# The Mamba-2 skip term moved from TensorE to VectorE and GpSimd, and product steps placed anew

## The chip, the cores and the metric

The kernel runs on one core of a Trainium2 chip. The metric is device time in microseconds (us) of one execution, the median of several runs. The core has TensorE (matmul, PE in the profile; its weight loads are PEld), VectorE (DVE), ScalarE (ACT), GpSimd (POOL) and SyncE (SP, which here only issues DMAs). TensorE writes its results to PSUM, eight banks here, and every other engine but GpSimd can read them there.

## The reference, cut to what matters

Two layers follow each other on 4096 tokens of width 256. The change lies in the first: a graph product (a 4096 x 4096 matrix of weights, computed from `dist_matrix`, times messages) and then a Mamba-2 block.

```python
weights = jnp.where(dist_matrix < CUTOFF, jnp.exp(-(1.0 / r - 1.0 / mu) ** 2 / (2.0 * sigma * sigma)), 0.0)
x = x + weights @ (z @ W + B)                       # the product of the first layer
...
zxbcdt = x @ W_in                                   # z, xBC and dt
xBC = jax.nn.silu(conv)                             # xh, Bmat, Cmat
...
Y = (Y_diag + Y_off + xh * D[:, None]).reshape(Bsz, L, D_INNER)
Y = Y * jax.nn.silu(z)
Y = Y * jax.lax.rsqrt(jnp.mean(Y * Y, axis=-1, keepdims=True) + EPS) * norm_w
return (Y @ W_out) @ W_lin + b_lin
```

The term `xh * D[:, None]` is the skip: each of the 512 channels of the convolved input times one constant of its head, added to what the recurrence gives.

## The kernel before

The tokens are worked in 8 blocks of 512 (`ib`), each block of the recurrence in 4 chunks of 128 tokens (`s`). The first layer overlaps three things in each block's time, in an order written out by hand (`order_a`, which every engine follows):

- `ssd(ib)`, the recurrence of block ib in 62 steps, with the output projection, a norm and the messages of the next layer behind it;
- `pre_a(ib + 1)`, norm, input projection and convolution of the next block, 55 steps;
- `product_a(ib + 2)`, the product for the block after that, 64 steps ("p") of one matmul each on TensorE. Its weights are made elsewhere ("w"): ScalarE takes a logarithm and two exponentials, VectorE does lines 1146 and 1153 on tiles of 128x1024, each line two at a time. Six tiles `wgt` form a ring.

Blocks 0 to 5 carry all 64 product steps. Block 6 carries 24 and block 7 carries 32 steps of the next layer's product, whose tiles need no such work. TensorE's "p" steps stand where `FILLS` puts them (pairs of an ssd step and a number of product steps ahead of it), and the rest are spread evenly up to ssd step 58:

```python
fill = [ssd_at[i] - 1e-6 for i, n in FILLS for _ in range(n)]
at += [(x, "p") for x in fill + spread(n_fill - len(fill), 0.02, ssd_at[SEND])]
```

One chunk of the recurrence has two parts, and on each engine `inner(s + 1)` stands ahead of `outer(s)`.

- `inner(s)`: TensorE transposes the convolved input into a PSUM bank `X` (785) and makes B transposed and B C in another (789, 791). VectorE takes `X` times dt into `xdt` (1251), copies `bn` (1254) and masks `cbm` (1256). ScalarE makes the decays `E` of 8 heads; GpSimd makes `xdec` (2190) and multiplies `E` by `cbm` (2195, its result is waited for as `M`).
- `outer(s)`: TensorE multiplies C by the state h0 (807, `Yo`), B by xdec (812, `St`), the four 128x128 blocks of the convolved input by diagonal matrices `diagD` that hold D (817, into `Y`), and adds E times xdt for 8 heads to the same bank (823). VectorE scales `Yo` into `tmp` (1266), adds `St` to `hd` for the new state h0 (1271), adds `Y` to `tmp` (1275) and multiplies by the gate z (1278); ScalarE squares that with a sum (1660). GpSimd makes `hd`, the decayed state (2207), from h0.

The state is a chain: 807 of chunk s + 1 waits for 1271 of chunk s, and GpSimd's 2207 of chunk s + 1 too. After the last chunk ScalarE makes the norm's factors `rms`, VectorE scales by them (1288, 1292), TensorE transposes (840) and projects (849).

PSUM banks are given out in rings in the order of use: `pre_a` has two banks, ps2 and ps3, so that each of its uses waits until the use two before it has been read. On TensorE, `pre_a` writes for each m an input part x (753, 755) and a gate part z (760, 762); ScalarE copies each out. Line 745 is the dt projection of `pre_a(ib + 1)`; it waits for the normed input `xc` (VectorE, 1201) and stands once in a block. GpSimd's 2153 adds the two halves of a later block's input, once a block. In the first rounds VectorE also writes `Wc` (1320) from a combination of two weight matrices (875).

## Time and profile before

| | us |
|---|---|
| median of 3 runs | 2359.17 |
| lowest, highest | 2358.28, 2360.71 |
| profiled execution, span of its instructions | 2358.5 |
| TensorE busy in the span | 2189.1 |
| VectorE, ScalarE, GpSimd busy | 1803.0, 1566.7, 1146.6 |

The span of the profiled execution is 0.67 us below the median of the runs. Times of the trace count from the span's start. The first layer's blocks run from about 230 to 1050 us; the second layer takes the rest. Busy time on TensorE is the union of its matmuls, whose modelled ends overlap: one product matmul, two instructions here, starts every 0.86 us, though each lasts 0.59. A block in the steady part is shown below by the stretch from one L745 at 459.5 us to the next at 571.9 us; the blocks around it repeat it.

### The profile page before, as it was taken

What the parts mean: (1) busy time and instruction counts of PE and PEld (TensorE: products, weight loads), DVE (VectorE), ACT (ScalarE), POOL (GpSimd) and SP (SyncE); (2) the same over time, 40 slices, a digit from 0 to 9 for tenths busy, and PEclk for the clock granted to TensorE, in tenths of its full rate; (3) what the DMA queues carried; (4) which work ended last, traced back from release to release, by engine and by line L of the source; (5) the groups of instructions that cost most, each with busy time, mean ns of one, the idle gap of its engine ahead of it and who ended that gap; (6) DMA issues with size and microseconds to landing.
All of it is one profiled execution on the core that took longest, in us unless ns stands there. A gap on an engine that the chain in (4) does not pass through costs nothing.

```text
span 2358.5 us, 26231 instructions
## 1 busy us (share of the span) xinstructions
PE 2189.1 (93%) x8900; PEld 1393.1 (59%) x8900; DVE 1803.0 (76%) x2083; ACT 1566.7 (66%) x2541; POOL 1146.6 (49%) x928
## 2 busy tenths in 40 slices
PE   7999999999999999989999999998999987787998
PEld 4544545555555556456766666676766664444886
DVE  5666767777777765324999998999989998996665
ACT  5577686777686845425676767677676868775444
POOL 2101322222231313213988888888988888890000
PEclk9999999999999999999999999999999999898999
DMA  6243332323232323233323232323323221312121
GB/s 234 72 134 102 108 116 90 125 96 122 87 125 88 119 90 134 83 107 109 131 93 125 90 125 89 117 99 107 117 100 125 90 83 43 117 36 98 36 81 45
DMA packets 117495, 241.22 MB, mean 102 GB/s; under 512 B 8770, under 2 KB 66370, under 8 KB 116978
## 3 DMA queue, kind: packets, MB, share of 16 engines
q1 hardware_dynamic: 108290, 207.14, 26.4%
q0 software_dynamic: 8528, 31.36, 3.8%
q8 instruction: 71, 1.16, 0.2%
q10 hardware_dynamic: 544, 1.05, 0.1%
q14 instruction: 62, 0.51, 0.1%
HBM read 219.20 MB, written 20.32 MB: 102 GB/s over the span
## 4 chain that ended last, share of the span: by engine, by line
PE 65%; ACT 10%; POOL 10%; DVE 10%; issue 5%; DMA 0%; ACTq 0%; DVEq 0%; POOLq 0%
PE ps L685 13%; PE ps L727 10%; POOL dB L2306 6%; PE ps L971 5%; DVE h L1473 3%; PE ps L849 2%; PE ps L823 2%; PE ps L955 2%; POOL acc L2288 2%; PE ps L709 2%; ACT ps L1659 2%; ACT L1657 1%; POOL du L2302 1%; PE ps L755 1%; PE ps L753 1%
## 5 line engine op out<-in xcount | busy, mean ns | idle before, releaser
L1473 DVE TENSOR_TENSOR_SCAN h<-ps,hst,dB 128x512 f32<-128x512 f32 x512 | 636.9, 1270 | 59.0 <-ACT ps L1659 50.5
L2306 POOL TENSOR_TENSOR dB<-du,bc 128x512 f32<-128x512 f32 x512 | 648.0, 1287 | 61.6 <-DVE h L1473 59.1
L685 PE MATMUL ps<-wgt,msg 128*128 128x512 f32 x1024 | 489.0, 598 | 2.1 <-DVE xb L1181 2.1
L1659 ACT ACTIVATE ps<-dt,cols 128x512 f32<-128x512 f32 x512 | 351.9, 692 | 181.1 <-DVE h L1473 178.8
L727 PE MATMUL ps<-raw,msg 128*128 128x256 f32 x1792 | 436.3, 379 | 0.9 <-ACT hb L1659 0.9
L971 PE MATMUL ps<-consts,h 128*128 128x128 f32 x2048 | 318.9, 281 | 70.7 <-DVE acc L1435 38.0
L971 PEld LDWEIGHTS ps<-consts,h 128*128 128x128 f32 x2048 | 251.6, 144 | 224.8 <-DVE acc L1435 73.4
L727 PEld LDWEIGHTS ps<-raw,msg 128*128 128x128 f32 x1792 | 324.0, 190 | 74.1 <-issue 42.1
L685 PEld LDWEIGHTS ps<-wgt,msg 128*128 128x128 f32 x1024 | 190.0, 192 | 206.2 <-issue 204.6
L1659 ACT ACTIVATE wgt<-wgt 128x1024 f32<-128x1024 f32 x256 | 257.9, 1046 | 51.9 <-DVE wgt L1146 50.5
L2288 POOL TENSOR_TENSOR acc<-acc,part 128x512 f32<-128x512 f32 x174 | 226.4, 1301 | 59.7 <-ACT part L1659 58.3
L1146 DVE SCALAR_TENSOR_TENSOR wgt<-wgt 128x1024 f32<-128x1024 f32 x128 | 174.4, 1403 | 54.6 <-ACT wgt L1659 54.6
L1435 DVE SCALAR_TENSOR_TENSOR acc<-ps,Ct,acc 128x512 f32<-128x512 f32 x267 | 193.6, 725 | 5.3 <-PE ps L971 5.2
L1153 DVE SCALAR_TENSOR_TENSOR wgt<-raw,wgt 128x1024 f32<-128x1024 f32 x128 | 167.3, 1348 | 17.9 <-ACT wgt L1659 17.9
L1659 ACT ACTIVATE wgt<-raw 128x1024 f32<-128x1024 f32 x128 | 129.0, 1045 | 24.1 <-PE ps L685 23.9
L2195 POOL TENSOR_TENSOR E<-E,cbm 128x1024 f32<-128x1024 f32 x32 | 81.4, 2545 | 108.4 <-ACT E L1659 108.3
L2226 POOL DMA_DIRECT2D tmp_x<-xb x8 | 5.6, 696 | 254.5 <-DVE xb L1298 254.5
L1659 ACT ACTIVATE part<-ps,Ct 128x512 f32<-128x512 f32 x174 | 117.8, 677 | 1.7 <-PE ps L971 1.5
L2313 POOL TENSOR_TENSOR sq<-sq 128x512 f32<-128x512 f32 x7 | 9.0, 1289 | 207.8 <-ACT sq L1659 207.8
L1660 ACT ACTIVATE tmp<-z 128x512 f32<-128x512 f32 x32 | 20.2, 630 | 130.8 <-DVE z L1278 130.8
L1659 ACT ACTIVATE g<-ps,b 128x512 f32<-128x512 f32 x64 | 43.1, 685 | 84.4 <-PE ps L1052 79.5
L1225 DVE SCALAR_TENSOR_TENSOR cc<-xbc,cols,cc 128x512 f32<-128x512 f32 x120 | 93.6, 780 | 3.1
(320 smaller groups left out, 3589.9 us busy)
## 6 DMA issues: line engine op xcount, KB each, us to landing
raw<-in_adjT SPq DMA_DIRECT2D x256, 512.0 KB, 3.4
bc<-tmp_bc SPq DMA_DIRECT2D x64, 512.0 KB, 4.6
E<-tmp_bc POOLq DMA_DIRECT2D x32, 512.0 KB, 4.1
xb<-in_xT POOLq DMA_DIRECT2D x8, 512.0 KB, 4.1
tmp_x<-xb POOLq DMA_DIRECT2D x8, 512.0 KB, 4.2
x<-tmp_x SPq DMA_DIRECT2D x8, 512.0 KB, 5.8
tmp_x<-x SPq DMA_DIRECT2D x8, 512.0 KB, 4.8
msg<-in_W SPq DMA_DIRECT2D x4, 1024.0 KB, 10.6
```

What stands on the lines that cost most here:

```text
L685: x = e.matmul(P[d][:, :], msg[:, j, d * 128:(d + 1) * 128], wgt[g % NW][:, l, :], start=j == 0, stop=j == NJ - 1)
L727: x = e.matmul(P[0][:, 256 * d:256 * d + 256], msg[:, j, d * 128:(d + 1) * 128], quarters(g)[:, l, :], start=j == 0 and d == 0, stop=j == ...
L971: i = e.transpose(b.ps[:, m * 128:(m + 1) * 128], hr[n % 3][:, m, s * 128:(s + 1) * 128], ident)
L1146: e.scalar_tensor_tensor(wgt[i % NW][:, :, :], wgt[i % NW][:, :, :], -2.0, wgt[i % NW][:, :, :], ALU.add, ALU.mult).then_inc(S("q"), 1)
L1153: e.scalar_tensor_tensor(wgt[i % NW][:, :, :], raw[i % 4][:, :, :], 1.0, wgt[i % NW][:, :, :], ALU.is_lt, ALU.mult).then_inc(S("wgt"), 1)
L1225: e.scalar_tensor_tensor(c, xbc[:, m, k:k + TB], col("cw0", 4 * m + k), c, ALU.mult, ALU.add).then_inc(S("conv"), 1)
L1435: e.scalar_tensor_tensor(acc[:, s, :], b.ps[:, :], c, acc[:, s, :], ALU.mult, ALU.add).then_inc(b.evac, 1)
L1473: e.tensor_tensor_scan(hr[n % 3][:, m, :], PS[4 + k % 2].t[:, :], dBr[k % 4][:, :], hst[:, n % 16, m:m + 1], ALU.mult, ALU.add).then_inc(S ...
L1659: return e.activation(out, in_, func, bias=bias, scale=scale)
L2195: e.tensor_tensor(E[c % 3][:, :, :], E[c % 3][:, :, :], cbms[s % 2][:, None, :].broadcast_to([128, 8, 128]), ALU.mult).then_inc(S("M"), 1)
L2288: e.tensor_tensor(acc[:, s, :], acc[:, s, :], part[HANDED[j] % 2][:, :], ALU.add).then_inc(S("summed"), 1)
L2306: e.tensor_tensor(dBr[k % 4][:, :], du[:, m, :], bcr[i % 3][:, n % 2, :], ALU.mult).then_inc(S("dB"), 1)
```

## The change

The skip no longer goes through TensorE. VectorE multiplies `X` in PSUM by a row `Drow` (128x512, D in every partition) into one of two tiles `skips`, in `inner(s)` ahead of `xdt`. GpSimd adds `tmp` to it in `outer(s)`, after `hd`, and waits for VectorE's 1266 to do so. VectorE's addition of `Y` then takes `skips` in place of `tmp` and waits for GpSimd. TensorE starts `Y` with the E matmuls. `Drow` is made once: one matmul of ones by the diagonal matrices and one copy, in the first rounds. The broadcast row of the messages' bias gets its own tile and DMA, whose room is used for the second skip tile later. `FILLS` puts 23 product steps at fixed places, where it put 16. One semaphore of the last stage is merged into another with the same waits.

```diff
-        rows = sb(cA, "rows", [128, NROW])
-        Bbc, dtb, Abc = rows[:, 0:256], rows[:, 256:288], rows[:, 288:296]
-        diagD = sb(cA, "diagD", [128, 4, 128])
+        rows = sb(cA, "rows", [128, NROW - D])
+        dtb, Abc = rows[:, 0:32], rows[:, 32:40]
+        Drow = sb(cA, "Drow", [128, 512])
...
+        skips = [skip0, sb(cA, "skip1", [128, 512])]
+        diagD = skip0[:, :].rearrange("p (m c) -> p m c", m=4)
...
-        FILLS, SEND, WFIRST, WLAST, EVAC, PREND = ((5, 3), (7, 2), (8, 2), (25, 2), (30, 2), (38, 2), (50, 2), (57, 1)), 58, 0.04, 0.925, 0.97, 0.95
+        FILLS, SEND, WFIRST, WLAST, EVAC, PREND = ((5, 3), (7, 2), (8, 3), (25, 2), (30, 2), (32, 2), (38, 4), (50, 3), (57, 2)), 58, 0.04, 0.925, 0.97, 0.95
... (TensorE, outer)
-                    w.wait_ge(S("setup"), 5)
                     w.wait_ge(Y.evac, Y.n - 1)
-                    for m in range(4):
-                        e.matmul(Y.ps[:, m * 128:(m + 1) * 128], cc[:, m, ts_], diagD[:, m, :], start=m == 0, stop=False,
-                                 skip_group_check=True)
                     yield
                     w.wait_ge(S("M"), 4 * ib + s + 1)
... (TensorE, first rounds, behind the four matmuls of Wc)
+                    b = drow_use()
+                    w.wait_ge(S("setup"), 5)
+                    w.wait_ge(b.evac, b.n - 1)
+                    e.matmul(b.ps[:, :], one, skip0[:, :], start=True, stop=True).then_inc(b.full, 1)
... (VectorE, inner)
+                    if c < 2:
+                        w.wait_ge(drow_use().evac, drow_use().n)
+                    e.tensor_tensor(skips[s % 2][:, :], X.ps[:, :], Drow[:, :], ALU.mult)
                     e.tensor_tensor(heads(xd[:, :]), heads(X.ps[:, :]), dt[:, 8 * s:8 * s + 8, None].broadcast_to([128, 8, 64]),
                                     ALU.mult).then_inc(X.evac, 1)
... (VectorE, outer)
-                    w.wait_ge(Yo.evac, Yo.n)
-                    e.tensor_tensor(tmp[:, :], tmp[:, :], Y.ps[:, :], ALU.add).then_inc(Y.evac, 1)
+                    w.wait_ge(S("skip"), c + 1)
+                    e.tensor_tensor(tmp[:, :], skips[s % 2][:, :], Y.ps[:, :], ALU.add).then_inc(Y.evac, 1)
... (VectorE, first rounds, behind the four writes of Wc)
+                    b = drow_use()
+                    w.wait_ge(b.full, b.n)
+                    e.tensor_copy(Drow[:, :], b.ps[:, :]).then_inc(b.evac, 1)
... (GpSimd, first DMAs)
-            e.dma_start(rows[:, :], t["rows"].broadcast_to([128, NROW])).then_inc(S("d_rows"), 16)
+            e.dma_start(rows[:, :], t["rows"][:, D:NROW].broadcast_to([128, NROW - D])).then_inc(S("d_rows"), 16)
+            e.dma_start(Bbc[:, :], t["rows"][:, 0:D].broadcast_to([128, D])).then_inc(S("d_rows"), 16)
... (GpSimd, outer, behind hd)
-                    yield from [None] * 5
+                    yield from (None, None)
+                    Yo = outer_use(ib, s, 0)
+                    w.wait_ge(Yo.evac, Yo.n)
+                    e.tensor_tensor(skips[s % 2][:, :], skips[s % 2][:, :], tmp[:, :], ALU.add).then_inc(S("skip"), 1)
+                    yield from (None, None, None)
```

TensorE around chunk 1 of a steady block, before. `ps2` is written by 770 and 771 (sums of dt); `ps3` is written by 753 (here the first half of the second input part of `pre_a`), and `ps7` is chunk 1's `Y`:

```order
L812 MATMUL ps6<-xdec1,bn1 128x512
L685 MATMUL ps0<-wgt3,msg 128x512
L770 MATMUL ps2<-sm1,consts 128x32 x3
L771 MATMUL ps2<-consts,sm1 128x128
L817 MATMUL ps7<-diagD,cc0 128x128 x4
L685 MATMUL ps1<-wgt3,msg 128x512
L753 MATMUL ps3<-xc,Win 128x512
L823 MATMUL ps7<-xdt1,E0 128x64 x8
```

The same place now (lines shifted by the change: 685 is 694, 753 is 762, 823 is 828):

```order
L821 MATMUL ps6<-xdec1,bn1 128x512
L779 MATMUL ps2<-sm1,consts 128x32 x3
L780 MATMUL ps2<-consts,sm1 128x128
L694 MATMUL ps1<-wgt3,msg 128x512
L762 MATMUL ps3<-xc,Win 128x512
L694 MATMUL ps0<-wgt3,msg 128x512
L828 MATMUL ps7<-xdt1,E0 128x64 x8
L764 MATMUL ps3<-xc,Win 128x512
```

Between the state's matmul of chunk 1 (812, now 821) and the input part (753, now 762) one product step and the diagonal matmuls are gone.

TensorE around chunk 2 and the state matmul of chunk 3 (807, now 816), before:

```order
L812 MATMUL ps7<-xdec0,bn0 128x512
L685 MATMUL ps0<-wgt0,msg 128x512
L817 MATMUL ps4<-diagD,cc0 128x128 x4
L685 MATMUL ps1<-wgt0,msg 128x512
L685 MATMUL ps0<-wgt0,msg 128x512
L685 MATMUL ps1<-wgt0,msg 128x512
L823 MATMUL ps4<-xdt0,E1 128x64 x8
L685 MATMUL ps0<-wgt1,msg 128x512
L807 MATMUL ps5<-hs0,cc0 128x512
```

And now:

```order
L821 MATMUL ps7<-xdec0,bn0 128x512
L694 MATMUL ps0<-wgt5,msg 128x512
L694 MATMUL ps1<-wgt5,msg 128x512
L694 MATMUL ps0<-wgt0,msg 128x512
L828 MATMUL ps4<-xdt0,E1 128x64 x8
L694 MATMUL ps1<-wgt0,msg 128x512
L694 MATMUL ps0<-wgt0,msg 128x512
L694 MATMUL ps1<-wgt0,msg 128x512
L816 MATMUL ps5<-hs0,cc0 128x512
L694 MATMUL ps0<-wgt1,msg 128x512
```

Four product steps stood between 812 and chunk 2's E matmuls and one between these and the state matmul of chunk 3; now three and three.

GpSimd from chunk 3's `xdec` to the first load of the next block, before:

```order
L2190 TENSOR_TENSOR xdec1<-xdt1,ecd 128x512
L2167 DMA tmp_bc<-turned 32x128
L2195 TENSOR_TENSOR E2<-E2,cbm1 128x1024
L2207 TENSOR_TENSOR hd<-hs0,ecd 64x512 x2
L2153 TENSOR_TENSOR rr<-xb1 128x512
L2161 DMA E0<-tmp_bc 128x1024
```

And now (2190 is 2206, 2195 is 2211, 2207 is 2223, 2153 is 2169; 2228 is the new addition):

```order
L2206 TENSOR_TENSOR xdec1<-xdt1,ecd 128x512
L2183 DMA tmp_bc<-turned 32x128
L2211 TENSOR_TENSOR E2<-E2,cbm1 128x1024
L2223 TENSOR_TENSOR hd<-hs0,ecd 64x512
L2228 TENSOR_TENSOR skip0<-skip0,tmp 128x512
L2223 TENSOR_TENSOR hd<-hs0,ecd 64x512
L2228 TENSOR_TENSOR skip1<-skip1,tmp 128x512
L2169 TENSOR_TENSOR rr<-xb1 128x512
L2177 DMA E0<-tmp_bc 128x1024
```

Each `hd` is followed by an addition into a skip tile; the last `hd` and the sum of the halves (2169) now stand behind it.

## Rows read from the trace of the kernel before

**Rows 1.** The page: busy shares, and TensorE's busy tenths in 40 slices.
```profile
PE 2189.1 (93%) x8900; PEld 1393.1 (59%) x8900; DVE 1803.0 (76%) x2083; ACT 1566.7 (66%) x2541; POOL 1146.6 (49%) x928
...
PE   7999999999999999989999999998999987787998
```

**Rows 2.** By stretch: length; busy us of PE, PEld, DVE, ACT, POOL; granted clock; DMA.
```profile
353.50:465.90 112.40, 110.16 (x387) 59.35 (x386) 83.73 (x101) 84.01 (x131) 27.63 (x22) 1.00 0.33 108
...
907.20:1044.00 136.80, 126.04 (x499) 72.61 (x498) 58.62 (x91) 51.53 (x117) 32.22 (x28) 0.99 0.22 74
```

**Rows 3.** Groups by line on TensorE: count, busy, mean ns, idle before.
```profile
L685 PE MATMUL ps<-wgt,msg 128*128 128x512 f32 x1024 | 489.0, 598 | 2.1 <-DVE xb L1181 2.1
...
L817 PE MATMUL ps<-diagD,cc 128*128 128x128 f32 x256 | 33.8, 275 | 0.0
```

**Rows 4.** TensorE in order of time, end of steady block: start, length, [idle].
```profile
541.25 1.13 PE L634 MATMUL ps<-tmp,consts 128*128 128x512 f32 x2 [1.14 <-DVE tmp L1303]
...
552.84 3.72 PE L861 MATMUL ps<-W,z 128*128 128x256 f32 x16 [1.02 <-DVE z L1312]
...
565.66 6.17 PE L685 MATMUL ps<-wgt,msg 128*128 128x512 f32 x14
571.91 1.95 PE L745 MATMUL ps<-Win,xc 128*128 128x8 f32 x16
```

**Rows 5.** The chain that ended last: start, length, work of each piece.
```profile
459.53 1.95 PE ps L745 x16
...
480.52 0.89 PE ps L817 x8
...
569.73 0.60 DVE xdt L1251
...
570.72 1.14 DVE xc L1201
...
571.91 1.95 PE ps L745 x16
```

**Rows 6.** VectorE in order of time, steady block 459.5 to 571.9.
```profile
493.87 1.53 DVE L1225 SCALAR_TENSOR_TENSOR cc<-xbc,cols,cc 128x512 f32<-128x512 f32 x2
495.32 0.68 DVE L1266 TENSOR_TENSOR tmp<-ps,ecd 128x512 f32<-128x512 f32 x1
496.23 4.47 DVE L1153 SCALAR_TENSOR_TENSOR wgt<-raw,wgt 128x1024 f32<-128x1024 f32 x2 [0.22 <-ACT wgt L1659]
500.62 0.67 DVE L1271 TENSOR_TENSOR hs<-hd,ps 64x512 f32<-64x512 f32 x1
...
506.09 2.36 DVE L1146 SCALAR_TENSOR_TENSOR wgt<-wgt 128x1024 f32<-128x1024 f32 x2 [0.19 <-ACT wgt L1659]
...
515.17 0.49 DVE L1288 TENSOR_SCALAR z<-z,rms 128x512 f32<-128x512 f32 x1 [1.26 <-ACT rms L1659]
```

**Rows 7.** GpSimd in order of time, same block.
```profile
494.84 2.78 POOL L2195 TENSOR_TENSOR E<-E,cbm 128x1024 f32<-128x1024 f32 x1 [2.79 <-ACT E L1659]
497.60 2.02 POOL L2207 TENSOR_TENSOR hd<-hs,ecd 64x512 f32<-64x512 f32 x1
...
502.48 1.27 POOL L2153 TENSOR_TENSOR rr<-xb 128x512 f32<-128x512 f32 x1
```

**Rows 8.** ScalarE, then three TensorE rows, same block.
```profile
479.92 0.58 ACT L1659 ACTIVATE z<-ps 128x512 f32<-128x512 f32 x1
...
482.11 1.02 PE L753 MATMUL ps<-xc,Win 128*128 128x512 f32 x2
...
503.66 1.02 PE L807 MATMUL ps<-hs,cc 128*128 128x512 f32 x2
...
517.50 0.60 PE L840 MATMUL ps<-consts,z 128*128 128x128 f32 x4
```

**Rows 9.** VectorE: a collision in block 6, then the first rounds.
```profile
926.55 3.83 DVE L1225 SCALAR_TENSOR_TENSOR cc<-xbc,cols,cc 128x512 f32<-128x512 f32 x1
...
37.25 0.48 DVE L1320 TENSOR_SCALAR Wc<-ps,cols 128x256 f32<-128x256 f32 x1 [1.16 <-PE ps L875]
37.65 2.35 DVE L1153 SCALAR_TENSOR_TENSOR wgt<-raw,wgt 128x1024 f32<-128x1024 f32 x2
```

More of the change, by code:

```diff
@@ L219, in build @@
         hd = sb(cA, "hd", [64, 512])
+        skip0 = sb(cA, "skip0", [128, 512])
+        cM = ExitStack()
+        Bbc = sb(cM, "Bbc", [128, D])
+        cM.close()
+        skips = [skip0, sb(cA, "skip1", [128, 512])]
+        diagD = skip0[:, :].rearrange("p (m c) -> p m c", m=4)
         cA.close()
@@ L271, in build @@
         lane_b = (ccs[0][:, 2:4, :], ccs[0][:, 4:6, :], xdecs[1][:, :])
-        ring_a, ring_b = Ring(PS[2:5], 6 * NB // 2), Ring(PS[5:8], 6 * NB // 2 + 4)
+        ring_a, ring_b = Ring(PS[2:5], 6 * NB // 2), Ring(PS[5:8], 6 * NB // 2 + 5)
         prod = [Ring(PS[0:1], 3 * NB + 1), Ring(PS[1:2], NB + 1)]
@@ L283, in message_use @@
             if ib % 2:
-                return ring_b.use(ib // 2 * 6 + (4 if ib > 1 else 0) + i)
+                return ring_b.use(ib // 2 * 6 + (5 if ib > 1 else 0) + i)
             return ring_a.use(ib // 2 * 6 + i)
@@ L288, in combined_use, with drow_use @@
             return ring_b.use(6 + m)
+        def drow_use():
+            return ring_b.use(10)
         def pre_use(ib, i):
@@ L436, in build @@
         over_a = [(prod[1].use(NB).full, prod[1].use(NB).n), (ssd_use(NB - 1, 27).evac, ssd_use(NB - 1, 27).n), (ssd_use(NB - 1, 31).evac, ssd_use(NB - 1, 31).n),
-                  (S("hd"), 4 * NB), (S("M"), 4 * NB), (S("xdec"), 4 * NB), (S("halo"), NB + 1),
+                  (S("hd"), 4 * NB), (S("M"), 4 * NB), (S("skip"), 4 * NB), (S("xdec"), 4 * NB), (S("halo"), NB + 1),
                   *((S(f"d_x2_{b}"), 16 * len(range(b, NB, 3))) for b in range(3)), (S("d_m2"), 16 * (NB - 2))]
@@ L822, in outer @@
                     for h in range(8):
-                        i = e.matmul(Y.ps[:, h * 64:(h + 1) * 64], Es[:, h, :], xd[:, h * 64:(h + 1) * 64], start=False,
-                                     stop=h == 7, skip_group_check=True)
+                        i = e.matmul(Y.ps[:, h * 64:(h + 1) * 64], Es[:, h, :], xd[:, h * 64:(h + 1) * 64], start=True,
+                                     stop=True)
                     i.then_inc(Y.full, 1)
@@ L1087, in mean_of_bias @@
                 b = end_use(2)
-                w.wait_ge(S("b2c"), 1)
+                w.wait_ge(S("b2c"), 2)
                 w.wait_ge(b.evac, b.n - 1)
@@ L1134, in messages @@
                 yield
-                w.wait_ge(S("d_rows"), 16)
+                w.wait_ge(S("d_rows"), 32)
                 for s in range(4):
@@ L1138, in messages @@
                     w.wait_ge(b.full, b.n)
-                    e.tensor_tensor(msg[:, 4 * ib + s, :], b.ps[:, 0:256], Bbc, ALU.add).then_inc(b.evac, 1)
+                    e.tensor_tensor(msg[:, 4 * ib + s, :], b.ps[:, 0:256], Bbc[:, :], ALU.add).then_inc(b.evac, 1)
                     yield
@@ L1574, in second_matrices @@
                 w.wait_ge(b_tw.evac, b_tw.n)
-                e.tensor_scalar(b2[:, 0, :], b2[:, 0, :], tw[:, 0:1], None, ALU.mult).then_inc(S("b2a"), 1)
-                w.wait_ge(S("b2a"), 1)
+                e.tensor_scalar(b2[:, 0, :], b2[:, 0, :], tw[:, 0:1], None, ALU.mult).then_inc(S("b2c"), 1)
+                w.wait_ge(S("b2c"), 1)
                 e.scalar_tensor_tensor(b2c[:, :], b2[:, 1, :], tw[:, 1:2], b2[:, 0, :], ALU.mult, ALU.add).then_inc(S("b2c"), 1)
@@ L1663, in _ @@
             e.dma_start(spots[1], t["xT"][:, :, TB:2 * TB]).then_inc(S("d_x0"), 16)
-            w.wait_ge(S("d_rows"), 16)
+            w.wait_ge(S("d_rows"), 32)
             act(Abc, Abc, ACT.Exp).then_inc(S("Aexp"), 1)
```

## The prediction

> **What bounds the kernel now.** I read the page first: TensorE is busy in 93% of the span and in nine tenths or more of nearly every slice of the first layer [rows 1]. Then busy time by stretch: in one steady block TensorE is busy 110.16 of 112.40 us at granted clock 1.00, VectorE 83.73, ScalarE 84.01, GpSimd 27.63 [rows 2]. Then TensorE in order of time: in that block it waits in two places only, 1.14 and 1.02 us [rows 4]. By those views TensorE is the bound of blocks 0 to 5, and matmuls taken from it should come off the block one for one. The chain of waits adds a warning: the block's anchor, L745, starts 112.38 us after the last one, and right behind VectorE's 1201 (570.72 + 1.14 = 571.86), while the product steps ahead of it end at 565.66 + 6.17 = 571.83 [rows 4, 5]. There two bounds coincide. So I walk VectorE, ScalarE and GpSimd through a block too, since each works in order and gains nothing by the change.
>
> **What comes off TensorE.** L817 has 256 instructions, 8 per chunk [rows 3], and one chunk's eight hold the chain for 0.89 us [rows 5]. That is 3.56 us per block, and 28.5 us for all eight blocks. FILLS takes nothing away: 64 steps remain 64. From the first output transposes (840) to the block's end the order is the same as before, so a block's length changes by what happens ahead of 840, and by L745.
>
> **VectorE ahead of L745.** The new multiply stands ahead of `xdt`, and reads one operand from PSUM as 1251 does, so I take 1251's 0.60 us on the chain [rows 5], plus its 0.05 of spacing: 0.65. For chunk 1 it comes between 1146 and 1201, with nothing to hide it, as the sum above shows. Cost: 0.65 us per block, six times. For chunk 0 VectorE waits for the transposes and ScalarE takes `xc` later; I cost that at nothing, at most another 0.65 if that cover is gone.
>
> **GpSimd's addition.** It reads two SBUF tiles of 128x512; its nearest row is 2153's, 1.27 us [rows 7]. GpSimd has the time, but not VectorE: 1153's pair lasts 4.47 us in [rows 6] and 2.35 in [rows 9]. In that stretch GpSimd's 2195 runs to 497.62 and 2207 takes 2.02 us [rows 7] for 64x512, and 4.47 is what one tile after 2195, then 2207, then the other tile would take: 497.6 - 496.23 + 1.1 + 1.0 + 1.1 = 4.57. Meanwhile 1266, with a PSUM operand, keeps its 0.68 beside 2195 [rows 6, 7]. So operations with all inputs in SBUF take turns on the two engines, and those with a PSUM input don't. Each addition may then hold VectorE up by 0 to 1.27 us: 0 where VectorE is at a PSUM read, 1.27 where it wants the turn.
>
> By the Trainium skill ("SBUF — State Buffer", "Who interferes with whom") GpSimd and a VectorE instruction with two SBUF inputs exclude each other for the whole instruction, and the first to issue holds the ports. The trace agrees in the 4.47. If each of the four additions of a block held VectorE up in full, that would be 5.1 us per block of VectorE's time by my 1.27.
>
> **The first uncovered wait.** TensorE now reaches the second input part (753) sooner: the diagonals of chunks 0 and 1 are gone (2 x 0.89) and two product steps stand elsewhere (2 x 0.86; seven of them take 6.01 us in [rows 4]), in all 3.5 us: 482.11 - 3.5 = 478.6 [rows 8]. It writes a bank whose former content ScalarE copies out from 479.92 to 480.5 [rows 8]. That copy stands at the end of ScalarE's own run of work, which begins behind VectorE's chunk 0 and doesn't see TensorE. So 753 waits to 480.5 or 480.8, some 2 us. From 753 to the state matmul of chunk 3 (807) TensorE had 21.55 us (503.66 - 482.11); there a diagonal set goes and a product step comes, 21.5. So 807 can't start before about 502.0, against 503.66 before. At most 1.6 us of 3.56 is left by then.
>
> **The second.** 807 also needs the state from 1271, which ended at 500.62 + 0.67 = 501.3 [rows 6]. What lies ahead of it on VectorE gets longer. The two multiplies of chunks 2 and 3 take 0.65 each, the first of them inside a wait. With the wait for GpSimd's addition at chunk 1, VectorE is 0.8 us late at the pair 1225 (493.87 before, so 494.7), and ScalarE, less delayed, lets GpSimd's 2195 come at 495.2 (494.84 before) [rows 6, 7]. Before, 2195 came while the second 1225 ran, and waited: 2.78 in place of 2.36. Now it comes while the first runs, and would go ahead of the second. Then 1225's second waits 2.35 us, 1266 follows at 498.5, and the pair 1153 takes its turns with `hd` and with the new addition: 1271 ends near 503.6. If the second 1225 still goes first, 1271 ends near 502.3. So 807 starts between 502.3 and 503.6, and the wait for the state eats nearly all the 3.5 us. The three product steps put there have been worked off by then.
>
> **The third.** Behind it `hd` of chunk 3 waits for the addition of chunk 2, and the addition of chunk 3 and the sum of the halves fall on the pair 1146 (506.09, 2.36 alone [rows 6]), which grows by up to 2 x 1.27. VectorE's scaling 1288 (515.17) moves to 517.9 to 518.4, and 840 (517.50) to 518.3 to 518.9 [rows 6, 8]. TensorE gets there at 518.2, so it waits up to 0.7 us. As the new order holds one product step more ahead of 840 and one less behind it (0.86 us), TensorE behind the second transposes stands where it stood, or up to 0.6 us later.
>
> **Sum for blocks 0 to 5.** Per block 0.65 (L745) and -0.05 to +0.6: +0.6 to +1.25 us. I take +0.9, the middle, because the turn of 1225 and 2195 hangs on 0.3 us. Six blocks: +5.4.
>
> **Blocks 6 and 7, and the start.** These have no `wgt` work, so VectorE is light (58.62 of 136.8 us, [rows 2]) and some of TensorE's gain arrives. In block 6 the state of chunk 3 hangs on a 1225 that takes 3.83 us beside GpSimd [rows 9], and stays there; behind it the last diagonal and the moved steps give about 1.8. In block 7 each chunk hangs on E, GpSimd and the state: about 1.0. In the first rounds the extra matmul (0.86) and copy (0.48, as 1320) stand between 1320 and 1153 on VectorE [rows 9]: +1.3. The second DMA of the bias row is issued by GpSimd 0.54 us later than the first and is hidden by the load of the inputs; 0.5 if not. The merged semaphore costs nothing.
>
> Sum: 5.4 - 1.8 - 1.0 + 1.3 = +3.9 us against the profiled span, 2358.5, gives 2362.4; the median of runs lies 0.67 above it: **2363.1 us**.
>
> **Rivals.**
> - *The gain comes through in part.* The turns fall well, 1271 ends near 501.3 and 840 isn't late. Then ScalarE's copy is the bound: -1.6 + 0.65 = -0.95 per block, or -2 if VectorE's chunk 0 also ends 1 us sooner. Six times, with -1.5 for the rest: 2351.9, down to 2346. For it: every wait so far was small, and the race is close. Against: the walk needs all turns to fall one way.
> - *The gain comes through whole.* TensorE is the only bound: -28.5 + 1.3, so 2332. Against: ScalarE's copy at 479.92, which nothing in the change moves.
> - *Slower by turns lost.* In [rows 9] a 1225 waits for two GpSimd operations in a row, 3.83 us. If the additions at chunks 2 and 3 do this to VectorE in each steady block, the loss there is one more operation, 1.27 to 2.4 us above mine: per block +2.2 to +3.3, six times +13 to +20, so 2371 to 2378. It decides as soon as 1271 of chunk 2 ends later than 503.7. By the rule cited above the holder keeps the ports for an instruction, and says nothing of who is next; it makes this no less likely.
> - *The change doesn't do what it says*: TensorE waits elsewhere for as long, and the length is the same to 1 us: 2359. That is inside my forecast's range.
>
> **How the numbers follow.** About 0.2% (4.7 us) can be told from no change. Forecast and its near side (2358 to 2367) 0.52; in part 0.24; whole 0.04; turns lost 0.20. Faster than 2354.5: 0.04 and most of the second case, 0.22. Slower than 2363.9: turns lost and nearly half of the forecast, 0.42. The rest, 0.36, is within 0.2%. The range of 8 in 10 leaves out the whole gain, the far end of the partial one and the far end of turns lost: 2350 to 2372.
>
> **What the profile after would show.** No 128x128 group of `diagD`; 32 multiplies of 0.69 and 32 additions of 1.27 or more. TensorE less busy per steady block by 3.5 us but not shorter: waits at the second input part (2 us, for ScalarE), at the state matmul of chunk 3 (1 to 2 us more, for 1271), at the first output transposes, and 0.6 at L745 for 1201. 1153 and 1225 longer in the mean. I am wrong if the distance of two L745 is under 111.5 us: then VectorE had slack that I didn't see, or the turns fell well; and wrong the other way if it is over 114.

## The result, and the profile after

| | before | after |
|---|---|---|
| median of 4 runs, us | 2359.78 | 2368.14 |
| lowest to highest, us | 2358.28 to 2360.71 | 2364.64 to 2370.41 |
| span of the profiled run, us | 2358.5 | 2362.7 |
| second L745 (L754 after) to the last, us | 666.9 | 675.4 |
| one steady block, us | 112.37 | 113.8 |

The ratio is 1.0037, with an interval of 1.0025 to 1.0049: the change makes the kernel 0.37% slower. The profiled run of after was its fastest, 2364.64 us; that its span is 2362.7 is because a run's time is 1.8 to 2.1 us above the span of its instructions, here and in every run below. In after the lines have moved: L745 is L754, L753 is L762, L807 is L816, L840 is L845, L1271 is L1283, L1201 is L1210, L1153 is L1162, L1225 is L1234, L2195 is L2211, L2207 is L2223. The new ones are L1262 (VectorE's multiply) and L2228 (GpSimd's addition).

The page of after, the busy shares and the shares of the chain; [rows 1] answer to the first line:

```profile
PE 2172.5 (92%) x8646; PEld 1364.9 (58%) x8646; DVE 1867.0 (79%) x2116; ACT 1567.6 (66%) x2541; POOL 1190.9 (50%) x961
...
PE 49%; ACT 15%; DVE 14%; POOL 14%; issue 7%; DMA 1%; DVEq 0%; ACTq 0%; POOLq 0%
```

TensorE's share of the chain is down to 49%, from 65% on the page of before; the other three engines have 43% between them, before 30%.

After, by stretch from one L754 to the next (us, busy us and count of PE, PEld, DVE, ACT, POOL, granted clock, DMA); they answer to [rows 2]:

```profile
235.49:348.61 113.12, 107.19 (x353) 55.45 (x353) 93.28 (x105) 84.00 (x132) 33.10 (x26) 1.00 0.33 107
462.42:576.26 113.84, 108.70 (x353) 56.19 (x353) 93.53 (x105) 84.17 (x132) 33.09 (x26) 0.99 0.32 107
576.26:690.02 113.76, 108.98 (x352) 56.14 (x352) 93.24 (x105) 84.15 (x132) 33.08 (x26) 0.98 0.32 107
```

TensorE has 32 records less in a block (353 against 385), yet its busy time fell by 1.2 to 1.5 us in the later two, and by nearly 3 us only in the first. The first is the one whose granted clock stayed at 1.00.

After, TensorE's groups by line between 235.49 and 910.84 (count, busy us, mean ns, idle before and what ended it):

```profile
L762 PE MATMUL ps<-xc,Win 128*128 128x512 f32 x60 | 33.0, 633 | 9.4 <-ACT z L1674 9.4
...
L816 PE MATMUL ps<-hs,cc 128*128 128x512 f32 x48 | 27.5, 657 | 3.4 <-DVE hs L1283 3.4
...
L845 PE MATMUL ps<-consts,z 128*128 128x128 f32 x96 | 13.8, 276 | 0.7
...
L754 PE MATMUL ps<-Win,xc 128*128 128x8 f32 x97 | 11.9, 257 | 3.4 <-DVE xc L1210 3.4
```

The same four had no idle time of note before (0.4 us in all, at L745). They wait where the prediction put the waits: for ScalarE's `z` copy, for the state, for `xc`. After, one steady block in order of time (start, length, [idle before]), TensorE first, then VectorE, then GpSimd; they answer to [rows 4], [rows 6] and [rows 7]:

```profile
576.26 1.95 PE L754 MATMUL ps<-Win,xc 128*128 128x8 f32 x16 [0.68 <-DVE xc L1210]
...
579.00 1.83 PE L694 MATMUL ps<-wgt,msg 128*128 128x512 f32 x2
580.63 1.91 PE L821 MATMUL ps<-xdec,bn 128*128 128x512 f32 x2
...
598.15 1.10 PE L762 MATMUL ps<-xc,Win 128*128 128x512 f32 x2 [0.96 <-ACT z L1674]
...
620.76 1.12 PE L816 MATMUL ps<-hs,cc 128*128 128x512 f32 x2 [0.86 <-DVE hs L1283]
...
635.81 1.09 PE L845 MATMUL ps<-consts,z 128*128 128x128 f32 x8
```

```profile
576.12 4.54 DVE L1162 SCALAR_TENSOR_TENSOR wgt<-raw,wgt 128x1024 f32<-128x1024 f32 x2
...
612.26 3.51 DVE L1234 SCALAR_TENSOR_TENSOR cc<-xbc,cols,cc 128x512 f32<-128x512 f32 x2
...
616.29 3.82 DVE L1162 SCALAR_TENSOR_TENSOR wgt<-raw,wgt 128x1024 f32<-128x1024 f32 x2
620.04 0.67 DVE L1283 TENSOR_TENSOR hs<-hd,ps 64x512 f32<-64x512 f32 x1
```

```profile
577.22 2.36 POOL L2211 TENSOR_TENSOR E<-E,cbm 128x1024 f32<-128x1024 f32 x1 [1.43 <-ACT E L1674]
579.55 2.02 POOL L2223 TENSOR_TENSOR hd<-hs,ecd 64x512 f32<-64x512 f32 x1
...
612.81 2.41 POOL L2211 TENSOR_TENSOR E<-E,cbm 128x1024 f32<-128x1024 f32 x1 [2.19 <-ACT E L1674]
...
616.63 1.26 POOL L2228 TENSOR_TENSOR skip<-skip,tmp 128x512 f32<-128x512 f32 x1
```

At 612 the pair L1234, 1.53 us in [rows 6], lasts 3.51, because L2211 comes at 612.81 and goes ahead of the second; L1162 behind it takes its turns with `hd` and with the addition. That is the late branch of the race at the second wait. At 576.12 the same happened where I had not looked: the multiply of 0.6 us ahead of L1162 lets GpSimd's L2211 in between its two instructions, and the pair takes 4.54 us, 2.35 before ([rows 9] have one that runs alone). Version 5 below, which leaves the multiply out, has 2.35 there again. By the Trainium skill ("SBUF — State Buffer", "Who interferes with whom") a VectorE instruction with two SBUF inputs contends with a GpSimd instruction that reads SBUF; the 4.54 us agree.

**What I did not foresee** is in the two rows behind L754. A pair of 128x512 matmuls takes 1.02 us in [rows 8]; here two pairs take 1.83 and 1.91. After, TensorE alone by short stretches: us, busy, granted clock, DMA:

```profile
578.70:582.40 3.70, 3.70 (x7) 0.55 0.54 158
483.50:487.00 3.50, 3.18 (x4) 0.51 0.02 5
```

The granted clock stands at 0.50, the 1.2 GHz level, for some 3.4 us; below this is called a fall. Through blocks 0 to 5, after has five such falls, one in each stretch from the second to the sixth: three start 1 to 3 us behind the 0.68 us wait at L754 (350, 579, 692), two right behind a wait of 2.2 us at L762 (483, 825). Before has none between 235 and 902.

### The profile page after: what moved, and what is told of

It reads as the page before. It is cut to its first block, busy times and chain, and to the rows that moved or that the text cites. A ratio compares the mean times of both kernels' runs of the same rounds, so it can differ in the third digit from the quotient of the medians.

```text
span 2362.7 us, 25802 instructions
## 1 busy us (share of the span) xinstructions
PE 2172.5 (92%) x8646; PEld 1364.9 (58%) x8646; DVE 1867.0 (79%) x2116; ACT 1567.6 (66%) x2541; POOL 1190.9 (50%) x961
## 4 chain that ended last, share of the span: by engine, by line
PE 49%; ACT 15%; DVE 14%; POOL 14%; issue 7%; DMA 1%; DVEq 0%; ACTq 0%; POOLq 0%
PE ps L736 10%; PE ps L694 7%; POOL dB L2326 6%; PE ps L980 5%; ACT wgt L1674 3%; DVE h L1488 3%; ACT E L1674 3%; PE ps L854 2%; DVE wgt L1162 2%; PE ps L964 2%; POOL E L2211 2%; POOL acc L2308 2%; ACT ps L1674 2%; ACT L1672 2%; DVE wgt L1155 2%
## 5 line engine op out<-in xcount | busy, mean ns | idle before, releaser
L1155 DVE SCALAR_TENSOR_TENSOR wgt<-wgt 128x1024 f32<-128x1024 f32 x128 | 196.4, 1575 | 46.3 <-ACT wgt L1674 46.3
L1162 DVE SCALAR_TENSOR_TENSOR wgt<-raw,wgt 128x1024 f32<-128x1024 f32 x128 | 176.0, 1416 | 10.6 <-ACT wgt L1674 10.2
L2211 POOL TENSOR_TENSOR E<-E,cbm 128x1024 f32<-128x1024 f32 x32 | 76.2, 2382 | 100.5 <-ACT E L1674 100.5
L1234 DVE SCALAR_TENSOR_TENSOR cc<-xbc,cols,cc 128x512 f32<-128x512 f32 x120 | 105.6, 880 | 3.1
```

The lines of the kernel that those rows point to most:

```text
L1155: e.scalar_tensor_tensor(wgt[i % NW][:, :, :], wgt[i % NW][:, :, :], -2.0, wgt[i % NW][:, :, :], ALU.add, ALU.mult).then_inc(S("q"), 1)
L1162: e.scalar_tensor_tensor(wgt[i % NW][:, :, :], raw[i % 4][:, :, :], 1.0, wgt[i % NW][:, :, :], ALU.is_lt, ALU.mult).then_inc(S("wgt"), 1)
L1234: e.scalar_tensor_tensor(c, xbc[:, m, k:k + TB], col("cw0", 4 * m + k), c, ALU.mult, ALU.add).then_inc(S("conv"), 1)
L2211: e.tensor_tensor(E[c % 3][:, :, :], E[c % 3][:, :, :], cbms[s % 2][:, None, :].broadcast_to([128, 8, 128]), ALU.mult).then_inc(S("M"), 1)
```

## Experiments

Two theories at the start. **A**: VectorE, ScalarE and GpSimd bound a block as soon as TensorE is relieved, so little of the 28.5 us could come through. **B**: TensorE is the bound and the change's own additions eat the gain. Single questions came with them: multiply or addition, the placement, the clock. All lengths below are of one block, L745 (L754) to the next, in the one execution of each version that was profiled. "At a full clock" means a granted clock of 1.00 throughout the block. Versions 1, 2, 5, 6 and 9 leave the skip, or a part of it, out of the result.

**1. The removal alone.**

```diff
-                    for m in range(4):
-                        e.matmul(Y.ps[:, m * 128:(m + 1) * 128], cc[:, m, ts_], diagD[:, m, :], start=m == 0, stop=False,
-                                 skip_group_check=True)
...
-                        i = e.matmul(Y.ps[:, h * 64:(h + 1) * 64], Es[:, h, :], xd[:, h * 64:(h + 1) * 64], start=False,
-                                     stop=h == 7, skip_group_check=True)
+                        i = e.matmul(Y.ps[:, h * 64:(h + 1) * 64], Es[:, h, :], xd[:, h * 64:(h + 1) * 64], start=True,
+                                     stop=True)
```

> The kernel before without its diagonal matmuls (L817) and with nothing in their place, all steps placed as before; the recurrence's skip is left out of the result. It asks what the removal alone could ever give. Theory A (the chain of ScalarE's z copy, VectorE's convolution and GpSimd's products bounds a block soon after TensorE is relieved): a block goes from 112.37 us to about 110.8, total near 2348 us, range 2344 to 2353. Rival B (TensorE alone bounds the stage): the whole 28.5 us come back, total near 2331 us. Rival C (waits take all of it): within 2 us of 2359.

Measured: 2336.14 us (2334.63 to 2338.74), ratio 0.9909 (0.9892 to 0.9925). One block by stretch, then its TensorE and ScalarE rows:

```profile
559.80:668.94 109.14, 106.84 (x353) 55.67 (x353) 83.30 (x101) 84.04 (x132) 27.97 (x22) 1.00 0.34 111
```

```profile
580.19 0.58 ACT L1656 ACTIVATE z<-ps 128x512 f32<-128x512 f32 x1
```

```profile
580.82 1.12 PE L753 MATMUL ps<-xc,Win 128*128 128x512 f32 x2
```

Theory A falls: 3.23 of 3.56 us a block come off. L753 does start at the very end of the `z` copy (580.77), as the prediction had it. The diagonals of chunks 0 and 1, 1.78 us, lie ahead of it, and 1.56 of them arrive: it starts 21.02 us behind its L745, against 22.58 before. The copy takes only some 0.2. Of the other two sets 1.67 come off behind it.

**2. The changed kernel without the addition.**

```diff
-                    e.tensor_tensor(skips[s % 2][:, :], skips[s % 2][:, :], tmp[:, :], ALU.add).then_inc(S("skip"), 1)
...
-                    e.tensor_tensor(tmp[:, :], skips[s % 2][:, :], Y.ps[:, :], ALU.add).then_inc(Y.evac, 1)
+                    e.tensor_tensor(tmp[:, :], tmp[:, :], Y.ps[:, :], ALU.add).then_inc(Y.evac, 1)
```

> The changed kernel without GpSimd's addition of the skip to tmp (L2228) and without its semaphore; VectorE adds tmp to the PSUM tile as before, its multiply (L1262) stays, and the skip is left out of the result. Theory A (the additions and the port turns that they take put L1283 and the halves of the next input late): the block falls from 113.8 us to about 111.5, the wait ahead of L816 of chunk 3 (0.86 us) shrinks, total near 2352 us. Rival D (the multiply ahead of L754 carries the loss): L754 is still late by 0.65 us a block, total 2362 to 2367. Rival E (the moved product steps carry it): total unchanged within 2 us of 2367.

Measured: 2352.88 us (2349.08 to 2357.95). Two blocks, one with a fall of the clock in it, one without:

```profile
458.00:570.04 112.04, 108.50 (x353) 56.32 (x353) 88.82 (x105) 84.06 (x132) 27.50 (x22) 0.98 0.33 108
683.02:794.41 111.39, 106.80 (x352) 55.71 (x352) 88.59 (x105) 84.05 (x132) 27.49 (x22) 1.00 0.33 109
```

The total is what was expected: by the medians the additions cost 15 us. The wait at L816 is gone (0.86 in after), the 0.68 at L754 stays. Two more blocks with a fall took 112.32 and 112.98.

**3. The multiply behind `xc`.**

```diff
-                    e.tensor_tensor(skips[s % 2][:, :], X.ps[:, :], Drow[:, :], ALU.mult)
...
                     e.tensor_tensor(cbms[s % 2][:, :], b.ps[:, 128:256], tri, ALU.mult).then_inc(b.evac, 1)
+                    yield from (None, None)
+                    e.tensor_tensor(skips[s % 2][:, :], X.ps[:, :], Drow[:, :], ALU.mult).then_inc(X.evac, 1)
```

> The changed kernel with VectorE's multiply (L1262) behind the pair's third step of the slot, so that in chunk 1 it stands behind the multiply into xc (L1210) on which L754 waits; the skip is computed whole. Theory A: the 0.68 us wait ahead of L754 goes, but the waits ahead of L762 (ScalarE's copy, 0.96 us) and of L816 of chunk 3 (0.86 us) are set elsewhere, so 0.3 to 0.65 us a block, total 2363 to 2366. Rival D (the multiply carries the loss): -1.4 us a block, total near 2358. Rival F (the fall of TensorE's granted clock to 0.50 behind that wait costs time): the fall vanishes with the wait and the total falls by 3.4 x 0.5 = 1.7 us in each of three blocks beyond Theory A, near 2360. If the waits behind swallow it: unchanged, 2367.

Measured: 2368.18 us (2364.23 to 2374.81, five runs; a sixth took 11181 us and is left out), 1.0045 (1.0029 to 1.0061): no gain. The wait at L754 is gone, but the one for the `z` copy behind it is 2.73 us, and the clock falls there:

```profile
462.71:578.95 116.24, 111.25 (x353) 58.42 (x353) 92.74 (x105) 84.25 (x132) 34.00 (x26) 0.96 0.32 104
578.95:691.96 113.01, 107.29 (x353) 55.54 (x353) 92.20 (x105) 84.13 (x132) 33.98 (x26) 1.00 0.33 107
```

Same kernel, same work: 3.2 us apart. In the longer block the clock stood at 0.50 for some 10 us, from 484 to 494, in the other not at all. So theory F, that the fall vanishes with the wait at L754, is wrong: it comes behind the next wait instead.

**4. The old placement.** The table of before in the changed kernel.

```diff
-FILLS = ((5, 3), (7, 2), (8, 3), (25, 2), (30, 2), (32, 2), (38, 4), (50, 3), (57, 2))
+FILLS = ((5, 3), (7, 2), (8, 2), (25, 2), (30, 2), (38, 2), (50, 2), (57, 1))
```

> The changed kernel with the product steps placed by the table of before (eight entries instead of nine). Theory A (the waits come from VectorE, ScalarE and GpSimd, the placement only fills TensorE's idle time): total 2366 to 2371, same or up to 3 us slower, the waits ahead of L816 and L845 open as idle time of TensorE. Rival E (the new placement itself puts convolution and transposes late): total falls to 2350 to 2358.

Measured: 2371.83 us (2370.22 to 2376.5). Blocks of 114.1 to 115.0 us, the second one at a full clock:

```profile
348.81:462.94 114.13, 107.32 (x352) 55.51 (x353) 93.40 (x105) 84.12 (x132) 33.08 (x26) 1.00 0.33 106
```

With the multiply and the additions there, the new placement is worth some 4 us in all.

**5. The changed kernel without the multiply** (from the third chunk on).

```diff
-                    e.tensor_tensor(skips[s % 2][:, :], X.ps[:, :], Drow[:, :], ALU.mult)
+                    if c < 2:
+                        e.tensor_tensor(skips[s % 2][:, :], X.ps[:, :], Drow[:, :], ALU.mult)
```

> The changed kernel with VectorE's multiply (L1262) run for the first two chunks alone; GpSimd's addition (L2228) stays for all 32 chunks, so the skip is wrong in the result from the third chunk on. The earlier runs gave for a steady block whose granted clock stays at 1.00: 109.1 us with nothing in the diagonal matmuls' place, 111.4 with the multiply and without the addition, 113.1 with both (first block of the changed kernel). Theory G (each of the two has its own price): multiply 2.3 us, addition 1.7 us, so 110.8 us a block and a total near 2348 us, and the wait ahead of L754 is gone. Theory H (the addition costs only behind the multiply, which takes VectorE's turn at the shared buffer port away): 109.3 us a block, total near 2338. Theory I (the addition carries nearly all of it): 112.5 or more, total 2358 or above.

Measured: 2363.10 us (2358.43 to 2368.36), nearest to theory I. Blocks of 113.1 to 113.2 us, each with a short fall of the clock, and two of 116. None is at a full clock, so the addition's price without the multiply is not told apart from that of the fall: both together cost 2.2 us a block over version 6. Two of them by stretch, then the fall in the second, then the row at which it starts:

```profile
461.30:574.40 113.10, 108.58 (x353) 56.27 (x353) 88.09 (x101) 84.01 (x132) 33.46 (x26) 0.98 0.33 107
574.40:690.36 115.96, 111.45 (x353) 58.43 (x353) 88.19 (x101) 84.14 (x133) 33.49 (x26) 0.96 0.32 105
595.40:605.80 10.40, 9.90 (x24) 6.08 (x25) 8.06 (x7) 4.11 (x9) 3.60 (x3) 0.52 0.01 2
```

```profile
595.90 2.05 PE L762 MATMUL ps<-xc,Win 128*128 128x512 f32 x2 [2.26 <-ACT z L1674]
```

The fall of the second block lasts some 10 us, from the wait at L762 on. The two blocks differ by 2.86 us.

**6. No skip, new placement.** As 1, with the table of after (the edit of 4 the other way round).

> The kernel before without its diagonal matmuls and with nothing in their place, as in e1_no_skip, but with the product steps placed by the table of after; the skip is left out of the result. If the placement does nothing without waits to fill: 2336 us within 2, a block of 109.1 us. If it is itself a burden (steps ahead of the convolution that VectorE waits for): 110 us a block or more, 2342 us or above. If it is a help everywhere: below 2334.

Measured: 2351.43 us (2341.37 to 2357.29). The profiled execution was the fastest:

```profile
564.76:675.67 110.91, 106.80 (x352) 55.71 (x353) 83.23 (x101) 83.91 (x132) 27.95 (x22) 1.00 0.33 109
```

```profile
585.87 1.10 PE L753 MATMUL ps<-xc,Win 128*128 128x512 f32 x2 [1.87 <-ACT z L1656]
```

So the placement, which takes two product steps from ahead of the `z` copy, by itself costs 1.77 us a block while nothing stands in the diagonals' place: TensorE waits 1.87 us for the copy that it had met within 0.2 in 1. And the ten runs scatter over 16 us, with mean clocks from 0.983 (2341.37) down to 0.974 to 0.976 (2352.89 to 2357.29). The four of 1 lie within 4.1 us.

**7. Blocks 6 and 7 alone**, **8. those and chunk 0.** Diagonal matmuls elsewhere, old placement; 8 returns `ib >= 6 or s == 0`:

```diff
+        def by_vector(ib, s):
+            return ib >= 6
...
+                    if not by_vector(ib, s):
+                        for m in range(4):
+                            e.matmul(Y.ps[:, m * 128:(m + 1) * 128], cc[:, m, ts_], diagD[:, m, :], start=m == 0, stop=False,
+                                     skip_group_check=True)
...
+                    if by_vector(ib, s):
+                        e.tensor_tensor(skips[s % 2][:, :], X.ps[:, :], Drow[:, :], ALU.mult)
```

> Diagonal matmuls in blocks 0 to 5, multiply and addition in blocks 6 and 7 alone, where no product steps run beside the recurrence; old placement; the skip is computed whole. The changed kernel took 4.8 us less than before from L754 of block 6 on. If that was the change's own gain there: blocks 0 to 5 as before (112.37 us), total 2353 to 2356 us, less a start that is up to 0.6 us later. If it came from something else (the placement, the state in which block 6 was reached): 2358 to 2360.

> As e7_tail_only, and in blocks 0 to 5 chunk 0 also takes the multiply and the addition, chunks 1 to 3 the diagonal matmuls; the skip is computed whole. Chunk 0's multiply stands 14.6 us ahead of L754, behind a 2.5 us wait of VectorE, its addition behind hd. If these two lie in idle time there: -0.81 us a block, total 5 us under e7_tail_only, 2348 to 2351. If the addition's turns at the port put L1283 or the halves behind it late, as in the changed kernel: equal to e7_tail_only or up to 5 us above it, 2354 to 2360.

Measured: 7, 2364.57 us (2360.94 to 2368.22), 1.0024 (1.0015 to 1.0034); 8, 2356.46 us (2352.95 to 2361.16), 0.9991 (0.9981 to 1.0001). 7 missed both of its ranges: from the last L745 to the first product matmul of the next layer it takes 151.7 us, against 151.9 before, though its diagonals are gone, and its total is 5 us above before. Of that its profile shows 2.3: 1.0 ahead of the second L757 (745 before), 1.2 in the second layer, nothing in blocks 0 to 5 (112.38). Why these two are longer stays open. Two waits for the state have their place (the two rows of 7); after had taken 147.6 there, 1 took 148.5 and 6 took 144.9, so a good part of that gain goes with the placement. In its blocks 8 did what was hoped (the last row, a steady one): 0.88 us less than 112.37, the whole of chunk 0's 0.89. Its total, 8 us under 7, stays above the 2348 to 2351 that were expected.

```profile
933.18 1.42 PE L819 MATMUL ps<-hs,cc 128*128 128x512 f32 x2 [2.40 <-DVE hs L1292]
...
1010.07 1.13 PE L819 MATMUL ps<-hs,cc 128*128 128x512 f32 x2 [2.55 <-DVE hs L1292]
```

```profile
570.84:682.33 111.49, 109.25 (x377) 58.44 (x377) 84.31 (x102) 84.02 (x132) 28.86 (x23) 1.00 0.32 109
```

**9. and 10. Waits filled with matmuls that nothing reads.** In 9 on the kernel of 6, 16 of them; in 10 on the changed kernel, 8 there and 6 more ahead of the wait at L754:

```diff
+                        for k in range(16):
+                            e.matmul(b.ps[:, 128:256], tri, tri, start=True, stop=True)
```

> e6_no_skip_new_placement (no skip at all, the table of after) with 16 matmuls of 128x128 on constants added ahead of L771, which nothing reads: 1.76 us of TensorE work in a place where it had waited 1.87 us for ScalarE's z copy (the wait ahead of L753). The skip is left out of the result. Ten runs of e6 lay between 2341 and 2357 us, at mean clocks from 0.983 down to 0.974. Theory W (TensorE's granted clock falls behind that wait in some of the executions, and that makes them longer): without the wait all runs lie within 5 us of each other, at 0.98 or more, median 2341 to 2345, though TensorE has 12 us more to do. Rival V (the clock falls for another reason): the scatter stays, median 2351 or above.

> The changed kernel, whole, with 6 such matmuls (0.66 us) ahead of the wait at L754 and 8 (0.88 us) ahead of L780, in front of the wait at L762. Theory W: the clock stays at 1.00 in blocks 0 to 5, the blocks take 113.1 us instead of 113.8, total 2362 to 2365 us. Rival V: a total of 2367 to 2371 with falls of the clock as before. Rival K (the added matmuls themselves put L762 and the halves late): 114 us a block at a clock of 1.00.

Measured: 9, 2363.02 us (2357.61 to 2364.29); 10, 2368.50 us (2365.94 to 2368.86, five runs). I had sized the filler by half: each of these matmuls shows as two records of 0.11 us, so 9 holds 3.5 us of them in each block, twice the wait, and 10 holds 1.3 and 1.8. The anchor of 10 is L756. A block of 9, then one of 10:

```profile
573.29:685.67 112.38, 110.14 (x385) 59.38 (x385) 83.25 (x101) 83.91 (x132) 27.93 (x22) 1.00 0.33 108
```

```profile
579.85:693.10 113.25, 110.11 (x383) 58.76 (x381) 93.39 (x105) 84.14 (x132) 33.06 (x26) 1.00 0.33 107
```

No fall of the clock stands between the second anchor and the last in either profile. For 10 that is a change from after's five; for 9 it shows nothing by itself, as the profile of 6, its fastest run, had none either, but nine of the ten runs of 9 lie within 3.5 us, all ten within 6.7 (6 had 16), at mean clocks of 0.979 and more. The block of 10 is 0.5 us shorter than after's with 3 us more on TensorE. The totals are no better: the filler is too large, and it also costs the stretch between the first two anchors 2.6 to 2.8 us. For 9 that leaves theory W half shown (the scatter shrank, the price of a fall is not seen in the total); for 10 the block met the expected 113.1, and the total missed the expected 2362 to 2365.

**11. and 12. A second chunk.** As 8 in blocks 0 to 5, with chunk 2 or chunk 3 besides, and diagonals in blocks 6 and 7:

```diff
-            return ib >= 6 or s == 0
+            return ib < 6 and s in (0, 2)
```

> In blocks 0 to 5 chunks 0 and 2 take the multiply and the addition, chunks 1 and 3 and all of blocks 6 and 7 the diagonal matmuls; old placement; the skip is computed whole. e8_tail_and_chunk_0 showed a steady block of 111.49 us (0.89 less than before: the whole price of one chunk's diagonal matmuls). If chunk 2's pair is also hidden (multiply 11 us behind L754, where VectorE waited 1.08 us; addition 40 us behind it): 110.6 us a block, total 2350 us. If the multiply or the addition puts L1283 or ScalarE's z copy late: 111.5 us or more, total 2355 or above.

> As e11, but with chunks 0 and 3 in blocks 0 to 5. Chunk 3's multiply stands 31 us behind L754, its addition 47.7 us behind it, where GpSimd had been idle for 2.2 us in the changed kernel, but beside the pair of products that L1300 and L845 wait for. Hidden: 110.6 us a block, total 2350 us. If the addition's turns reach L845 (1.9 us of slack in the kernel before): 111.5 us or more, total 2355 or above.

Measured: 11, 2352.42 us (2348.43 to 2357.84), 0.9978 (0.9968 to 0.9988); 12, 2358.62 us, 1.0001 (0.9992 to 1.0011). A block of 11; then one of 12, the wait that 12 has in addition, and the pair of VectorE ahead of it:

```profile
566.61:677.63 111.02, 108.62 (x369) 57.45 (x369) 86.31 (x103) 84.03 (x132) 30.40 (x24) 1.00 0.33 110
```

```profile
571.79:683.64 111.85, 108.58 (x369) 57.47 (x369) 86.98 (x103) 83.91 (x132) 30.15 (x24) 1.00 0.33 108
```

```profile
629.16 0.66 PE L854 MATMUL ps<-consts,z 128*128 128x128 f32 x4 [1.03 <-DVE z L1312]
```

```profile
617.46 4.46 DVE L1164 SCALAR_TENSOR_TENSOR wgt<-wgt 128x1024 f32<-128x1024 f32 x2 [0.18 <-ACT wgt L1686]
```

Chunk 2 gives 0.47 us of its 0.89. Chunk 3 costs 0.36 more than it takes away: the pair L1164, 2.36 us in [rows 6] (1146), takes 4.46 beside GpSimd's addition (617.35) and its sum of the halves (618.59), and L1312 (1288 before), for which TensorE waits, comes behind it. The total of 12 doesn't show the 0.5 us a block that it still gains: its profiled run was its slowest, 2365.36, and took 6.8 us more than before in the second layer, whose work no version changes. Version 11 computes the whole skip and is faster than both kernels, over before by a margin that is barely past what can be told.

## Where the time went

At a clock of 1.00 throughout, a block takes, in us:

| kernel | block | step |
|---|---|---|
| before | 112.37 | |
| 1: no skip | 109.14 | removal -3.23 |
| 6: and new placement | 110.91 | +1.77 |
| 2: and multiply | 111.39 | +0.48 |
| after | about 113.25 | addition +1.86 |
| after, with one fall of the clock a block | 113.8 | about +0.55 |

The steps are those of this order of building up; in another order a part can cost something else. The fifth line rests on two blocks, since each of after's steady blocks has a fall. One is the first block of after, 113.12 us at a clock of 1.00. Its L754 starts without a wait, 0.28 us behind VectorE's L1162; in the steady blocks, which start with a wait for VectorE, it is 0.14 (576.26 against 576.12). Counted from VectorE, from this L1162 (235.21) to the one a block later (348.48), it took 113.27:

```profile
235.49 1.85 PE L754 MATMUL ps<-Win,xc 128*128 128x8 f32 x16
```

```profile
235.21 4.53 DVE L1162 SCALAR_TENSOR_TENSOR wgt<-raw,wgt 128x1024 f32<-128x1024 f32 x2
```

The other is the block of 10, 113.25. Both are 0.85 to 0.9 above before, and both leave 0.5 to 0.6 for a fall.

By chunks, at a full clock and all with the old placement: chunk 0 gives -0.88 (8), chunk 2 -0.47 (11), chunk 3 costs 0.36 (12), and all four together cost 114.13 - 112.38 = 1.75 (4). What is left for chunk 1 is 1.75 + 0.88 + 0.47 - 0.36 = +2.74. That is a remainder, and assumes that the chunks add up; no run has chunk 1 alone. It is the chunk whose multiply stands ahead of L754 and whose addition comes 23.8 us behind it, beside two products. The new placement takes 0.88 off the four together.

## The prediction, point by point

- **TensorE's relief**, 0.89 us per chunk: right. Run 1 gives 3.23 of 3.56 a block, and 8 gives 0.88 for one chunk.
- **"At most 1.6 us of 3.56 is left by then."** Right for the new placement (6 has 1.44 left at the L807 of chunk 3, 42.69 us behind its anchor against 44.13 before), wrong as a statement about the removal (1 has 2.36, 41.77). I took the 3.5 us ahead of L753 as one sum, two sets of diagonals and two moved steps. With the steps left in place 1.56 of the diagonals' 1.78 us arrive there, and the copy takes 0.2 (1). ScalarE was hardly a bound on the gain; the placement made it one (6, a wait of 1.87).
- **The multiply ahead of L745**, 0.65: the wait is there, 0.68. It can't be taken away alone (3), since the next wait grows.
- **The first wait**, some 2 us for the `z` copy: 2.09 in the first block, 2.16 and 2.17 in two later ones, 0.96 to 1.00 where the clock had fallen ahead of it.
- **The second**: L807 of chunk 3 between 502.3 and 503.6. It came 44.50 us behind its block's L754, which is 504.0 counted from 459.53, 0.4 past the late end. The race of 1225 went the late way. In the first block, at a full clock, it is 43.85, or 43.99 counted from VectorE as above, which is 503.5, inside.
- **The third**: 840 at 518.3 to 518.9. It came at 59.55, which is 519.1; in the first block at 58.90, or 59.04 counted from VectorE, which is 518.6, inside, and 1.07 later than before. The wait of up to 0.7 us there did not come; L845 has 0.7 us in all six stretches. With 0.86 us of product steps less behind it and the 0.65 at L745, the sum is +0.86 a block.
- **Sum for blocks 0 to 5**: +5.4 predicted; measured +0.85, 1.43, 1.46, 1.39, 1.44 and 1.84, in all 8.4. This is the term that was too small: five of the six lie above its range of +0.6 to +1.25. The first, the only one without a fall, lies inside it, and by the table a steady block at a full clock does too, at about +0.87 against the +0.9 that was taken. So the walk through the engines was right for what it walked through. What it had at nothing is the clock, about +0.55 in each block with a fall.
- **Start**: +1.3 predicted, +0.6 at the second L754; versions 2 to 5, with nearly the same start, have -0.6 to +0.9, so one profile doesn't settle it. **Blocks 6 and 7**: -2.8 predicted, -4.3 in the profile up to the next layer, and another -0.5 behind it, where the work is the same. 7 shows that the reason given, TensorE's gain arriving in light blocks, is not enough: with the new path there and the old placement nothing arrives.
- **The total**: predicted 2363.1, measured 2368.1, with a profiled span of 2362.7 against the 2362.4 of the sum. That agreement is partly luck: the 3.0 us that blocks 0 to 5 took above their sum are nearly made up by the 2.7 that the start and the rest took below theirs. The median of after lies 3.5 us above the time of its profiled run. The sum had taken the 0.67 of before, whose profiled run was one of its slower ones. Why the other three runs of after took 2.3 to 5.8 us more is not shown: their mean clocks, 0.976 and 0.977, are as good as that of the profiled one, 0.977.
- **Rivals.** The slower one, turns lost, was priced at +2.2 to +3.3 a block and did not come: L1283 of chunk 2 ends at 620.71, 503.98 in the old frame, 0.3 past the point from which it was to decide, but with one operation lost and not two. Its total, 2371 to 2378, lies above all runs of after. "Whole gain" fails by every line of the table, and 1.77 us of that is the `z` copy that was held against it, together with the placement. "In part", -0.95 a block, is what 2 has at a full clock (111.39, -0.98): it fails by the additions.

## To carry to other kernels

When an engine that is busy 98% of a block is relieved, leave out the work and put nothing in its place before arguing what else would bound it: here that gave 22 us, where the walk through the other engines had left less than half of 3.56 a block. Try an order of work by itself too: the one that was chosen to help cost 1.77 us a block on its own and gave 0.88 beside the new work. Then price the replacement piece by piece and place by place, for a multiply of 0.6 us was free in one chunk and let another engine's 2.4 us operation in ahead of a pair in the next. And count a new wait of TensorE dearer than its length where the trace shows the clock falling behind it.
